# Order of the linear attention's middle part against the expert choice, in a fused transformer block on one NeuronCore

## What is computed

```python
mod = (silu(c) @ wmod).reshape(4, 6, 1, 256)          # sa, ca, ga, sb, cb, gb
h = layernorm(x) * (1 + ca) + sa
q, k, v = h @ Wq.T, h @ Wk.T, h @ Wv.T; q, k = rope(q), rope(k)
kv = einsum('bshd,bshe->bhde', k, v); ksum = k.sum(1); vsum = v.sum(1)
num = einsum('bshd,bhde->bshe', q, kv) * scale + vsum
den = einsum('bshd,bhd->bsh', q, ksum) * scale + 1024
o = num / den + depthwise_conv5(v)
x = x + ga * ((o * (h @ Wg.T)) @ Wo.T)
h = layernorm(x) * (1 + cb) + sb
p = softmax(h @ router.T); idx = top_k(p + bias, 6); w = p[idx] / sum(p[idx])
y = sum over 6 experts of w * (silu(gate) * up) @ down, and one shared expert
x = x + gb * y
```

## Time and profile before

| | |
|---|---|
| median of 3 runs | 886.05 us (885.17 to 888.2) |
| the profiled execution's own time | 886.46 us |
| its span, first to last instruction | 884.3 us |
| mean granted TensorE clock (1 is full speed) | 0.942 |
| PE busy | 790.0 us (89%) |
| DVE busy | 527.5 us (60%) |
| ACT busy | 430.2 us (49%) |
| POOL busy | 413.9 us (47%) |
| a block load of 160 KB, from issue to landing | 2.7 us in the median |
| the chain that ended last | PE 61%, DVE 18%, DMA 7%, issue 5% |

### The profile page before, as it was taken

One profiled execution on the slowest core, in us unless ns is written; L12 is line 12 of the kernel. 1 busy time (PEld: TensorE's weight loads), 2 busy tenths in 40 slices (PEclk: granted clock), 3 DMA queues, 4 the chain that ended last, 5 costly groups with the idle time before them and its releaser, 6 DMA issues.

```text
span 884.3 us, 17213 instructions
## 1 busy us (share of the span) xinstructions
PE 790.0 (89%) x4232; PEld 597.6 (68%) x4233; DVE 527.5 (60%) x1412; ACT 430.2 (49%) x1125; POOL 413.9 (47%) x420
## 2 busy tenths in 40 slices
PE   3897898898799898989998998899999999989964
PEld 3445557565764754759987877799999999845521
DVE  1576698679859976654444444444454445445664
ACT  5353456283262415317765665677777777500000
POOL 0000000077657767745777777776666666600000
PEclk9899997799799779899999999999999999999988
DMA  9300001033323598564767777777656664299981
GB/s 329 110 0 1 0 1 48 2 125 139 139 77 125 191 360 300 203 230 145 222 217 244 240 247 247 229 224 242 192 159 190 187 191 133 52 318 365 355 291 48
DMA packets 100725, 157.34 MB, mean 178 GB/s; under 512 B 14378, under 2 KB 80047, under 8 KB 100528
## 3 DMA queue, kind: packets, MB, share of 16 engines
q1 hardware_dynamic: 76464, 95.68, 34.6%
q0 software_dynamic: 19968, 56.67, 17.5%
q10 hardware_dynamic: 4224, 4.19, 1.4%
HBM read 87.10 MB, written 73.56 MB: 182 GB/s over the span
## 4 chain that ended last, share of the span: by engine, by line
PE 61%; DVE 18%; DMA 7%; issue 5%; ACT 4%; POOL 4%; DVEq 0%; SPq 0%; ACTq 0%; POOLq 0%
PE ps_wide L1030 16%; PE ps_wide L1038 8%; DMA expert_outs<-arena,dest 6%; PE ps_wide L823 6%; PE ps_narrow L1079 6%; PE ps_wide L735 5%; PE ps_narrow L1019 4%; PE ps_wide L831 4%; PE ps_kv L764 3%; POOL expert_outs L463 3%; PE ps_narrow L938 2%; DVE arena L1187 2%; DVE arena L1309 2%; PE ps_wide L944 2%; PE ps_narrow L905 2%
## 5 line engine op out<-in xcount | busy, mean ns | idle before, releaser
L449 POOL DMA_INDIRECT expert_rows<-arena,slot_i x192 | 196.0, 1021 | 245.8 <-ACT arena L601 184.9
L463 POOL DMA_INDIRECT expert_outs<-arena,dest x224 | 217.7, 972 | 113.1 <-issue 66.5
L1030 PE MATMUL ps_wide<-arena 128*128 128x128 f32 x1792 | 239.2, 277 | 2.2 <-ACT arena L646 2.2
L1030 PEld LDWEIGHTS ps_wide<-arena 128*128 128x128 f32 x1792 | 219.8, 194 | 2.7 <-ACT arena L646 2.5
L658 ACT COPY arena<-arena 128x512 f32 x224 | 138.3, 618 | 38.0 <-PE ps_kv L764 11.6
L1470 DVE TENSOR_TENSOR arena<-arena,ps_wide 128x128 f32<-128x128 f32 x224 | 64.5, 288 | 151.1 <-ACT arena L652 77.4
L1038 PE MATMUL ps_wide<-arena 128*128 x448 | 136.7, 387 | 10.6 <-DVE arena L1470 10.5
L646 ACT COPY arena<-ps_narrow 128x256 f32<-128x256 f32 x224 | 83.2, 372 | 81.4 <-PE ps_narrow L1019 79.7
L1478 DVE TENSOR_SCALAR arena<-ps_wide,arena 128x256 f32<-128x256 f32 x224 | 107.6, 481 | 2.1 <-PE ps_wide L1038 1.7
L823 PE MATMUL ps_wide<-arena 128*128 128x512 f32 x192 | 87.8, 605 | 5.1 <-DVE arena L1187 5.1
L1019 PE MATMUL ps_narrow<-cst,arena 128*128 128x128 f32 x448 | 86.7, 276 | 4.5 <-DMA arena<-expert_rows 4.5
(11 more groups left out here) (191 smaller groups left out, 957.9 us busy)
## 6 DMA issues: line engine op xcount, KB each, us to landing
arena<-expert_rows SPq DMA_DIRECT2D x224, 160.0 KB, 2.7
arena<-expert_outs SPq DMA_DIRECT2D x48, 512.0 KB, 9.3
arena<-w_experts SPq DMA_DIRECT2D x32, 384.0 KB
expert_rows<-pad_row SPq DMA_DIRECT2D x33, 160.0 KB, 7.2
x<-x SPq DMA_DIRECT2D x4, 1024.0 KB, 11.0
out<-x ACTq DMA_DIRECT2D x8, 512.0 KB, 7.3
expert_outs<-arena,dest POOLq DMA_INDIRECT x224
h_cols<-arena SPq DMA_DIRECT2D x6, 512.0 KB, 4.0
```

The lines of the kernel that those rows point to most:

```text
L449: nc.gpsimd.indirect_dma_start(rows, bass.IndirectOffsetOnAxis(ap=slots_i[b % 2][:, t, k:k + 1], axis=0), hrows[b % 2][:, t, :], None, bou ...
L463: nc.gpsimd.indirect_dma_start(outs, bass.IndirectOffsetOnAxis(ap=dest[:, u:u + 1], axis=0), yb[:, u, :], None, bounds_check=last_out, oob ...
L1030: last = mm(ps_wide[:, 0, u % 2, half * P:(half + 1) * P], wgu[:, u % 4, first:first + I], xbt[:, u % 2, c * P:(c + 1) * P], start=(c == 0 ...
```

## The change

The masked k-v products move into `choose()`, between `match_replace` and the mask, in the three `hurry` rounds. On PE the first two numerators go among the denominators, one ahead of each four tiles. The other two are issued before the transpose, and `rank()` stands between them. ACT waits for each numerator by itself. On DVE the inverse comes ahead of `take_ranks()`, and the spread ahead of `slots()`.

```diff
--- before.py
+++ after.py
@@ -619,8 +619,8 @@
                     act.wait_ge(s_vsum, b + 1)
 
                     for hf in range(HALVES):
-                        act.wait_ge(s_num, b * HALVES + hf + 1)
                         for m in range(C):
+                            act.wait_ge(s_num, (b * HALVES + hf) * C + m + 1)
                             src = ps_kv[:, m] if hf else ps_wide[:, 1, m]
                             last = nc.scalar.activation(num[:, hf, m], src, ACT.Identity, bias=vsum[:, m:m + 1])
                         last.then_inc(s_numc, 1)
@@ -926,24 +926,10 @@
                             last = mm(ps_kv[:, c, 0:P + 1], k_sb[:, t, c * P:(c + 1) * P], v_sb[:, t, c, 0:P + 1],
                                       start=(t == 0), stop=(t == TILES - 1))
                     last.then_inc(s_kv, 1)
-                if hurry:
-                    rank()
-                if front:
-
-                    pe.wait_ge(s_kvm, b + 1)
-                    if back:
-                        pe.wait_ge(s_lgm, b)
-                    for t in range(TILES):
-                        for c in range(C):
-                            last = mm(ps_narrow[:, 0, t * H + c * HC:t * H + (c + 1) * HC], qt[:, c, t * P:(t + 1) * P],
-                                      ksm[:, c, :], start=True, stop=True)
-                    last.then_inc(s_den, 1)
-                if front:
-                    def numerators(hf):
-                        for m in range(C):
-                            last = mm(ps_kv[:, m] if hf else ps_wide[:, 1, m], kvm[:, m, :],
-                                      qt[:, m, hf * HALF:(hf + 1) * HALF], start=True, stop=True)
-                        last.then_inc(s_num, 1)
+                if front:
+                    def numerator(hf, m):
+                        mm(ps_kv[:, m] if hf else ps_wide[:, 1, m], kvm[:, m, :],
+                           qt[:, m, hf * HALF:(hf + 1) * HALF], start=True, stop=True).then_inc(s_num, 1)
 
                     def broadcast(hf):
                         for m in range(C):
@@ -951,11 +937,22 @@
                                       rden_x[:, hf * TPH:(hf + 1) * TPH, :], start=True, stop=True)
                         last.then_inc(s_rdb, 1)
 
-
-                    numerators(0)
+                    pe.wait_ge(s_kvm, b + 1)
+                    if back:
+                        pe.wait_ge(s_lgm, b)
+                    for t in range(TILES):
+                        if t % TPH == 0:
+                            numerator(0, t // TPH)
+                        for c in range(C):
+                            last = mm(ps_narrow[:, 0, t * H + c * HC:t * H + (c + 1) * HC], qt[:, c, t * P:(t + 1) * P],
+                                      ksm[:, c, :], start=True, stop=True)
+                    last.then_inc(s_den, 1)
+                    numerator(1, 0)
+                    if hurry:
+                        rank()
+                    numerator(1, 1)
                     pe.wait_ge(s_rden, b + 1)
                     nc.tensor.transpose(ps_narrow[:, 0, 0:P], rden, ident).then_inc(s_rdt, 1)
-                    numerators(1)
                 if tabled:
                     count(0, ps_narrow)
                 if back and not hurry:
@@ -1229,6 +1226,27 @@
                     link(v.tensor_reduce(mx, lg, AX_X, ALU.max))
                     v.tensor_tensor(logit, lg, mx[:, :, None].to_broadcast(wide), ALU.subtract).then_inc(s_lgm, 1)
 
+                def mask_kv():
+
+                    dve.wait_ge(s_kv, b + 1)
+                    for c in range(C):
+                        v.tensor_tensor(kvm[:, c], ps_kv[:, c, 0:P], kv_mask, ALU.mult)
+                        last = v.tensor_scalar(ksm[:, c], den_mask, ps_kv[:, c, P:P + 1], None, ALU.mult)
+                    last.then_inc(s_kvm, 1)
+
+                def invert_den():
+
+                    dve.wait_ge(s_den, b + 1)
+                    den = rden[:, 0:TILES * H]
+                    link(v.tensor_scalar(den, ps_narrow[:, 0, 0:TILES * H], float(S), None, ALU.add))
+                    v.reciprocal(den, den).then_inc(s_rden, 1)
+
+                def spread_rden():
+
+                    dve.wait_ge(s_rdt, b + 1)
+                    v.tensor_tensor(rden_x, ps_narrow[0:TILES * H, 0:1, 0:P].to_broadcast([TILES * H, TILES, P]),
+                                    tile_mask[:, :, None].to_broadcast([TILES * H, TILES, P]), ALU.mult).then_inc(s_rdx, 1)
+
                 def choose():
 
                     dve.wait_ge(s_exp, b)
@@ -1246,6 +1264,8 @@
                     for t in range(TILES):
                         last = v.match_replace(left[:, t, :], top8[:, t, :], score[:, t, :], MARK)
                     link(last)
+                    if hurry:
+                        mask_kv()
                     link(v.tensor_scalar(mask, left[:, :, 0:E], MARK, None, ALU.is_equal))
                     for t in range(TILES):
                         last = v.tensor_tensor(seen[:, t + 1, :], seen[:, t, :], mask[:, t, :], ALU.add)
@@ -1356,34 +1376,24 @@
 
                 if follows and not first:
                     norm_next()
-                if front:
-
-                    dve.wait_ge(s_kv, b + 1)
-                    for c in range(C):
-                        v.tensor_tensor(kvm[:, c], ps_kv[:, c, 0:P], kv_mask, ALU.mult)
-                        last = v.tensor_scalar(ksm[:, c], den_mask, ps_kv[:, c, P:P + 1], None, ALU.mult)
-                    last.then_inc(s_kvm, 1)
+                if front and not hurry:
+                    mask_kv()
                     if first:
                         norm_next()
+                if back and not hurry:
+                    choose()
+                if front:
+                    invert_den()
+                    if first:
+                        convolve(range(2, 3))
                 if hurry:
                     take_ranks()
-                    slots()
-                elif back:
-                    choose()
-                if front:
-
-                    dve.wait_ge(s_den, b + 1)
-                    den = rden[:, 0:TILES * H]
-                    link(v.tensor_scalar(den, ps_narrow[:, 0, 0:TILES * H], float(S), None, ALU.add))
-                    v.reciprocal(den, den).then_inc(s_rden, 1)
-                    if first:
-                        convolve(range(2, 3))
-
-                    dve.wait_ge(s_rdt, b + 1)
-                    v.tensor_tensor(rden_x, ps_narrow[0:TILES * H, 0:1, 0:P].to_broadcast([TILES * H, TILES, P]),
-                                    tile_mask[:, :, None].to_broadcast([TILES * H, TILES, P]), ALU.mult).then_inc(s_rdx, 1)
+                if front:
+                    spread_rden()
                     if first:
                         convolve(range(3, TAPS))
+                if hurry:
+                    slots()
                 if tabled:
                     count_blocks(0, ps_narrow)
                 if not front:
```

## The result

The changed kernel is slower. Its runs have a median of 902.32 us (898.24 to 911.8, 4 runs), and those of the kernel before, taken again beside them, 887.12 us. The ratio is 1.0157, with a 95% interval of 1.0105 to 1.0209. By the ratio the loss is 13.9 us, by the medians 15.2. The profiled execution took 900.39 us, 13.9 us more than the one of the kernel before. Its span is 898.6 us.

A forecast was written before the change was run, and what follows sets the result against it. The page's chain (61% PE, 18% DVE), each step waiting for the last, was taken as the bound. Batch terms summed to +8.3 us at full clock, +22.1 with four falls; about half falling gave +15, 901.5 us, range 893 to 908.5.

The forecast's parts named there:

- The slots between spread and multiplication: Rounds 1 and 2: first multiplication waits for the slots, 15.7 us behind PE's start at full clock, 19.85 with a fall.
- PE's start: Rounds 1 and 2: earlier masked products let PE start 1.3 us earlier; no gain in round 3.
- Clock in the mixture: Numerators among denominators: clock falls in about half the batches; rivals: stays up (+8.3 us, 14%), falls in all (+22.1, 17%).
- Round 0: First multiplication behind two added numerators: at 96.85, +3.3 us with the clock's fall, +1.9 at full clock.
- Round 3: `count` waits for the slots and holds up the broadcasts: net +4.6 us at full clock, +8.8 with a fall.
- L831 directly follows busy broadcasts, so its slow start goes: Round 3's output projection: no idle time ahead of it, so 1.3 us comes back, 1.6 at most.
- Output projection of rounds 1 and 2: PE idles 4.9 us instead of 1.25 ahead of it, so it runs slower: +1.7 us each.
- Block loads: Experts' loads behind round 3's later slots: hidden by 5.8 us spare; rival, up to 3 us more, 904.5 us, 6%.
- The sum: All four batches: +8.3 us at full clock, +22.1 with falls everywhere; falls in about half taken, +15.

The follow-up runs named there:

- e2: The kernel before with only VectorE's order changed in rounds 1 to 3 (inverse, ranks taken, spread, slots); ratio 1.0114, median 903.08 us.
- v1: The changed kernel with round 0 in its old order and the slots cut in two, weights and orders ahead of the inverse; ratio 0.9951, median 884.63 us.
- e6: The changed kernel with three unused extra matmuls in TensorE's idle time ahead of the output projection in rounds 1 and 2; ratio 1.0165.
- e4: The changed kernel with round 0 put back in the order of the kernel before; ratio 1.0136, median 902.01 us.
- e8: The kernel before with numerators among the denominators in rounds 1 to 3, the second pair staying behind the transpose; ratio 1.0053, median 890.92 us.
- e1: The changed kernel with the slots of rounds 1 to 3 moved behind the output's first addition; ratio 1.0209, median 909.13 us.
- e3: The kernel before with numerators among the denominators in rounds 1 to 3, all four ahead of the transpose; ratio 1.0114, median 898.93 us.
- v3: As v1 without the mixture: all denominators, two numerators, ranks, transpose, two numerators; ratio 0.995, median 884.95 us.

## Why the prediction was right

The forecast was +15 us (901.5). The result is +13.9 us by the ratio, +13.9 between the two profiled executions, and +15.2 by the medians. The direction, the place of the cost and its rough size were worked out. That the number is met so closely is in part luck, since some terms were too small by what others were too large (the last point below).

- *The slots between spread and multiplication.* As forecast: L1413 follows them with no idle time, 15.06 us behind PE's start in round 2, where the clock stayed up in the mixture (forecast 15.7), and 20.07 us in round 1, where it fell (19.85). The denominators ended 5.45 us behind PE's start in round 2 and 8.2 in round 1, a little outside the 5.5 to 7.5 given. e2 and v1 show that this place is the main cost.
- *PE's start.* I took it 1.3 us earlier in rounds 1 and 2 and said that batch 1 has the same hand-overs. Counted from the end of the k-v sums, it was 2.5 us earlier in round 2 (0.92 against 3.39) and 0.3 us later in round 1 (2.75 against 2.45), where VectorE's `match_replace` ended 1.9 us behind the sums instead of 0.3. The two misses nearly cancel.
- *Clock in the mixture.* I took a fall in half of the batches. It fell in rounds 0 and 1 and not in 2 and 3. The page of the Trainium skill ("TensorE: Matmul & The Clock Gate", "What's actually happening"), by which activity releases the throttle, agrees with rounds 2 and 3 only; wide matmuls among the small ones did not hold the clock in the other two.
- *Round 0.* Forecast 96.85 for a fall as before; 96.82 measured. The output stretch gave 1.2 us back, which I had not counted: the broadcasts were slow instead of the projection.
- *Round 3.* `count` waits for the slots, and the first multiplication stands 19.29 us behind PE's start at 319.67 (forecast 19.75). The step "L831 directly follows busy broadcasts, so its slow start goes", -1.3 us, failed. It took 5.95 us, 0.6 more than before, since the broadcasts ahead of it were themselves at half clock.
- *Output projection of rounds 1 and 2.* The sign was right and the size was too small: 1.7 us each forecast, 2.8 us measured (6.54 and 6.45 against 3.70). The reason I gave was an idle time of 4.9 us, worked out with broadcasts at full clock. In this profile that step failed: the idle time was 1.61 us in round 1 and 1.42 in round 2. The clock had fallen earlier, in the broadcasts, and stayed low. e6 shows that the projection is fast once the clock is back. The way that I described occurs too: with 4.60 us idle in round 2 of e4 and 3.19 in e2 the projection took 6.36 and 6.22 us, behind broadcasts at full clock. What makes the clock fall in the broadcasts of one execution and not of another is not shown: in e8 it was up with numerators over the spread (projection 3.70), and in v1 it was up with nothing over the spread.
- *Block loads.* They stayed hidden, as forecast. e1 shows that the cover was not large: when the slots of round 3 ended 15.8 us behind the multiplication (346.1 against 330.3) instead of just ahead of it, PE waited 10.54 us.
- *The sum.* For falls in rounds 0 and 1 alone my terms give 3.3 + 5.0 + 0.9 + 4.6 = 13.8 us; the same stretches measured +16.4. The projections of rounds 1 and 2 (2.2 too small) and that of round 3 (2.0 too small) are the mis-sized terms. The middle of round 1 was 1.8 above its term and that of round 2 1.8 below, round 3's 0.5 below, and the output of round 0 gave 1.2 back. Outside these stretches 2.1 us came back, 1.7 of it between round 3 and the experts, where the clock was 0.94 against 0.91. I had no term for that.

What stays open: the parts alone make +1.1% (VectorE's order), +1.1% (the mixture) and +0.7% (the products), and the whole only +1.6%. They may share costs (the ranks that wait for the mask are gone in the whole, and low clock in the broadcasts could be paid once), but I have not separated these. And why the mixture costs 1% in e3 and nothing in v1 against v3 is not shown. In v1's profile the broadcasts of rounds 1 and 2 ran at full clock with the same idle time ahead of them.

## What to carry to other kernels

When work is moved out of the way of a critical result, ask what it stood under. Here 5.7 us of side work lay free under the denominators, and moving it behind the spread put it on the path in three rounds, in the third also ahead of another engine's wait. It pays to cut such a block by what each part needs: the 4.6 us that needed no ranks went back under the denominators, and the rest lay under the first broadcast. And on TensorE a step is priced with the clock that the engine has when it gets there: the projections of rounds 1 and 2 did the same work and took 2.8 us longer, whether the clock had fallen in the broadcasts (the changed kernel) or in the idle time ahead of the projection (e2, and round 2 of e4).

## What the runs showed of the hardware

- The small matmuls follow the clock just as the wide ones do, though 4 columns give them hardly anything to multiply. The chain of the changed kernel, in round 1 at 0.50 and in round 2 at 1.00 (start, duration, engine, output, line, records):

```profile
162.28 3.21 PE ps_narrow L947 x16
165.48 1.91 PE ps_kv L931 x2
...
242.14 1.68 PE ps_narrow L947 x16
243.82 0.96 PE ps_wide L931 x2
```

The 16 denominators went from 1.68 us to 3.21, two wide matmuls from 0.96 to 1.91.
- A low clock can outlast 10 us of work without a gap. In round 1 of the changed kernel each window of half a microsecond from 159.8 to 169.8 us shows 0.50, with PE busy in all of it. In round 2 it was 0.50 from 252.0 to 265.5 us, in the broadcasts, the transposes and most of the projection, and PE was busy but for 1.42 us. Why it stays low is not shown: the same broadcasts ran at full clock (3.70 us) in v1 and in round 2 of e4.
- Runs of one program differ with the clock that it was granted: v1 reached from 877.84 us (mean clock 0.959) to 890.78 (0.932), v3 only from 881.95 to 886.95, with a median 0.3 us away.
